# Source scan by flat scans: TensorE lays rows by feature in PSUM, GpSimd spreads flags, ScalarE spreads limits and turns rows back, VectorE scans

## The reference, cut to what matters

```
out = segment_sum(exp(-w)[:, None] * x[dst], src)      # layer 0: 64 features an edge
seg_sum = segment_sum(edge_attr_32, src)               # layer 1: 32 features an edge
seg_max = segment_max(edge_attr_32, src)               #          the same 32, maximum
h = relu(concat([seg_sum, seg_max, seg_mean, u]) @ W1 + b1) @ W2 + b2
```

## Time and profile before

| | us |
|---|---|
| median of 3 runs (9801.57 to 9804.97) | 9802.26 |
| the profiled execution | 9794.14 |
| its span | 9792.4 |
| its source scan (first flag comparison to last maximum, 2398.69 to 3061.24) | 662.5 |

### The profile page before, as it was taken

One profiled execution on the slowest core, in us unless ns is written; L12 is line 12 of the kernel. 1 busy time (PEld: TensorE's weight loads), 2 busy tenths in 40 slices (PEclk: granted clock), 3 DMA queues, 4 the chain that ended last, 5 costly groups with the idle time before them and its releaser, 6 DMA issues.

```text
span 9792.4 us, 48931 instructions
## 1 busy us (share of the span) xinstructions
PE 1437.4 (15%) x7747; PEld 1261.9 (13%) x7747; DVE 3669.9 (37%) x13437; ACT 2688.1 (27%) x3610; POOL 6744.4 (69%) x6983
## 2 busy tenths in 40 slices
PE   7544444441002200000001000000001000000000
PEld 6443333441001200000000000000001000000000
DVE  9766666664996311111111111111114222222225
ACT  0566666662000222222221222222220111111110
POOL 6677777775003577777777777777777777777775
PEclk6655555555555555555555555555555555555555
DMA  7445554454774122222222222222221222222222
GB/s 269 131 146 149 149 146 144 147 149 131 274 273 154 45 54 52 52 52 54 52 52 51 48 52 52 54 52 52 52 54 35 60 63 63 63 66 63 63 64 48
DMA packets 573558, 913.40 MB, mean 93 GB/s; under 512 B 335117, under 2 KB 351380, under 8 KB 547976
## 3 DMA queue, kind: packets, MB, share of 16 engines
q1 hardware_dynamic: 349752, 652.54, 20.0%
q0 software_dynamic: 223040, 258.35, 13.0%
q10 hardware_dynamic: 528, 0.15, 0.0%
HBM read 496.53 MB, written 414.02 MB: 93 GB/s over the span
## 4 chain that ended last, share of the span: by engine, by line
POOL 67%; issue 23%; DVE 7%; SPq 1%; DMA 1%; PE 1%; ACT 0%; DVEq 0%; POOLq 0%; ACTq 0%
POOL arena_a L690 45%; POOL by_src L638 16%; POOL arena_a L657 4%; DVE arena_a L1394 2%; DVE arena_a L1399 2%; POOL x_at_start L617 1%; SPq L415 1%; POOL adst_at_start L671 1%; DMA adst_at_start<-arena_a 0%; PE banks L1028 0%; DVE hrows L1284 0%; DVE cap_blk L1356 0%; DVE cap_blk L1357 0%; PE banks L952 0%; PE banks L1002 0%
## 5 line engine op out<-in xcount | busy, mean ns | idle before, releaser
L690 POOL DMA_INDIRECT arena_a<-table_c,decay x3136 | 2959.8, 944 | 1040.3 <-issue 954.8
L638 POOL DMA_INDIRECT by_src<-arena_b,idx_blk x1568 | 1555.4, 992 | 509.0 <-issue 476.7
L690 POOL DMA_INDIRECT arena_a<-table_at,decay x1568 | 1490.3, 950 | 477.8 <-issue 477.8
L1617 DVE COPY banks<-arena_a 128x64 f32<-128x64 f32 x194 | 52.7, 272 | 3346.3 <-ACT banks L753 3346.3
L753 ACT ACTIVATE banks<-arena_a 128x1024 f32<-128x1024 f32 x196 | 369.6, 1886 | 2999.0 <-DMA arena_a<-table_c,decay 2999.0
L733 ACT ACTIVATE arena_b<-same_dst 128x1024 f32<-128x1024 f32 (+1 forms) x294 | 312.9, 1064 | 1692.3 <-DVE arena_a L1755 1569.8
L742 ACT ACTIVATE arena_a<-arena_a 128x1024 f32<-128x1024 f32 (+1 forms) x294 | 597.9, 2034 | 3.9 <-DVE arena_a L1755 2.0
L976 PE MATMUL banks<-ident,chunk_end 128*64 128x128 f32 (+2 forms) x8 | 2.7, 442 | 3964.0 <-DVEq L1085 3964.0
L853 ACT ACTIVATE arena_b<-arena_a,decay 128x64 f32<-128x64 f32 x1568 | 468.1, 388 | 423.0 <-DMA by_src<-arena_b,idx_blk 423.0
L1710 DVE TENSOR_TENSOR arena_a<-arena_a 128x64 f32<-128x64 f32 x98 | 27.0, 275 | 1355.1 <-DMA arena_a<-table_at,decay 1355.1
L976 PEld LDWEIGHTS banks<-ident,chunk_end 128*64 128x64 f32 (+2 forms) x8 | 1.4, 239 | 3964.7 <-DVEq L1085 3964.7
(11 more groups left out here) (290 smaller groups left out, 5215.2 us busy)
## 6 DMA issues: line engine op xcount, KB each, us to landing
arena_a<-ids_rows SPq DMA_DIRECT2D x98, 1024.0 KB, 9.1
states_src<-arena_a SPq DMA_DIRECT2D x98, 1024.0 KB, 4.8
states_c<-arena_a SPq DMA_DIRECT2D x196, 512.0 KB, 2.6
hrows<-by_src SPq DMA_DIRECT2D x98, 776.0 KB, 6.1
states_at<-arena_a SPq DMA_DIRECT2D x98, 576.0 KB, 3.1
x_at_start<-arena_a SPq DMA_DIRECT2D x7, 7168.0 KB
arena_a<-x_at_start SPq DMA_DIRECT2D x98, 512.0 KB, 6.4
arena_a<-table_c,decay POOLq DMA_INDIRECT x3136, 2.4
```

What stands on the lines that cost most here:

```text
L638: pool.indirect_dma_start(out=by_src, out_offset=AT(ap=idx_blk[r][:, k:k + 1], axis=0), in_=rows[r][:, k, :], in_offset=None)\
L690: pool.indirect_dma_start(out=gb[r][:, k * w:(k + 1) * w], out_offset=None, in_=table[g], in_offset=AT(ap=src_i[:, n * J + k:n * J + k + 1 ...
```

## The change

The slots' chain of small steps becomes two flat scans a block, and four engines share the work:

- **TensorE** multiplies the block by the identity in four matmuls of 512 columns, whose operand is read with the slots inside and a step of 97 numbers between them. So a block lies in PSUM by feature, 128 features of 16 slots: 96 to sum, and the 32 attributes once more for the maxima. Two blocks fill the eight banks.
- **GpSimd** spreads the block's 15 flags over 96 features (`flags`, two buffers).
- **ScalarE** makes the caps, spreads them over 32 features (`caps_at`, two buffers), and behind the scans copies the block from `outs` (by feature, two buffers) to `runs` (by row, four buffers); it raises `state` now.
- **VectorE** compares the flags of the next block, puts the carries into slot 0 in PSUM, and scans 1536 and 512 elements.
- **SyncE** loads when a block's maxima are scanned and stores two blocks behind.

The diff, cut to its core:

```diff
+        def turned_src(h):
+            return banks[:, h * J * W01:(h + 1) * J * W01]
+        def slots_of(flat):
+            return flat.rearrange("p (f j) -> p f j", j=J)
...
+        late = carve(arena_a, [*((f"run{h}", J * W01) for h in range(R)), *((f"out{h}", J * W01) for h in range(2))])
+        late = carve(arena_b, [(f"flags{h}", J * WS) for h in range(2)] + [(f"caps{h}", J * E32) for h in range(2)])
...
@@ SyncE @@
                 for h in range(blocks):
                     if more:
                         if later(i) or h >= 2:
-                            sp.wait_ge(s("state"), i * R + h - 1)
+                            sp.wait_ge(s("src_maxed"), i * R + h - 1)
                         load(*((i, h + 2) if h < 2 else (i + 1, h - 2)))
-                    if later(i) or h:
-                        write_src(i * R + h - 1, (h - 1) % 2)
+                    if later(i) or h >= 2:
+                        write_src(i * R + h - 2, (h - 2) % R)
             def write_src(b, h):
                 sp.wait_ge(s("state"), b + 1)
                 sp.dma_start(rows_of(states["src"], W01)[:, bass.ds(b * (J * W01), J * W01)],
-                             st[h][:, 0:J * W01]).then_inc(s(f"stored{h}"), 16)
+                             runs[h][:, :]).then_inc(s(f"kept{h}"), 16)
...
@@ GpSimd @@
+            for n in range(NBLK):
+                pool.wait_ge(s("src_same"), n + 1)
+                if n >= 2:
+                    pool.wait_ge(s("src_summed"), n - 1)
+                pool.tensor_copy(slots_of(flags[n % 2])[:, :, 1:J], bf(mask_blk[:, n % 2, 1:J], WS))\
+                    .then_inc(s("src_spread"), 1)
...
@@ ScalarE @@
+            def caps_src(i, h):
+                q = h % 2
+                act.wait_ge(s("src_same"), i * R + h + 1)
+                if later(i) or h >= 2:
+                    act.wait_ge(s("src_maxed"), i * R + h - 1)
+                act.activation(cap_blk[:, q, :], mask_blk[:, q, :], ACT.Copy, bias=-1.0, scale=2.0)\
+                    .then_inc(s("cap_signs"), 1)
+                act.wait_ge(s("cap_signs"), i * R + h + 1)
+                act.activation(cap_blk[:, q, :], cap_blk[:, q, :], ACT.Copy, scale=HUGE).then_inc(s("src_capped"), 1)
+                act.wait_ge(s("src_capped"), i * R + h + 1)
+                act.activation(slots_of(caps_at[q])[:, :, 1:J], bf(cap_blk[:, q, 1:J], E32), ACT.Copy)\
+                    .then_inc(s("caps_spread"), 1)
+            def back_src(i, blocks=R):
+                for h in range(blocks):
+                    if h < R - 1 and (blocks == R or h < blocks - 1):
+                        caps_src(i, h + 1)
+                    elif blocks == R:
+                        caps_src(i + 1, 0)
+                    if later(i):
+                        act.wait_ge(s(f"kept{h}"), i * 16)
+                    rows = runs[h].rearrange("p (j f) -> p j f", f=W01)
+                    done = slots_of(outs[h % 2]).rearrange("p f j -> p j f")
+                    act.wait_ge(s("src_summed"), i * R + h + 1)
+                    act.activation(rows[:, :, 0:WS], done[:, :, 0:WS], ACT.Copy)
+                    act.wait_ge(s("src_maxed"), i * R + h + 1)
+                    act.activation(rows[:, :, WS:W01], done[:, :, WS:W01], ACT.Copy).then_inc(s("state"), 1)
+            caps_src(0, 0)
+            turns(act, back_src, TURNS)
+            back_src(TURNS, REST)
...
@@ TensorE @@
+            def turn_src(i, blocks=R):
+                for h in range(blocks):
+                    pe.wait_ge(s(f"tb_in{h}"), i * 16 + 16)
+                    if later(i) or h >= 2:
+                        pe.wait_ge(s("src_maxed"), i * R + h - 1)
+                    to = turned_src(h % 2)
+                    for b, f in enumerate((0, E32, D, D)):
+                        last = pe.matmul(to[:, b * J * E32:(b + 1) * J * E32], ident[:, :],
+                                         tb[h][:, :, f:f + E32].rearrange("p j f -> p f j"), start=True, stop=True)
+                    last.then_inc(s("src_turned"), 1)
...
@@ VectorE @@
+            for h in range(2):
+                link(v.memset(slots_of(flags[h])[:, :, 0:1], 0.0))
+                link(v.memset(slots_of(caps_at[h])[:, :, 0:1], -HUGE))
+            tell("src_same")
             def body(i, blocks=R):
                 for h in range(blocks):
...
+                    q, n = h % 2, (h + 1) % R
+                    if blocks == R or h < blocks - 1:
+                        v.wait_ge(s(f"tb_in{n}"), (i + (h + 1) // R) * 16 + 16)
+                        if later(i) or h:
+                            v.wait_ge(s("src_spread"), i * R + h)
+                            v.wait_ge(s("caps_spread"), i * R + h)
+                        for ins in same_src(n, tb[h][:, J - 1, TW - 1:TW]):
+                            pass
+                        ins.then_inc(s("src_same"), 1)
+                    v.wait_ge(s("src_turned"), i * R + h + 1)
+                    if later(i) or h:
+                        sums, maxima = (slots_of(turned_src(q))[:, f, 0] for f in (slice(0, WS), slice(WS, W01)))
+                        old = slots_of(outs[1 - q])
+                        v.wait_ge(s("src_summed"), i * R + h)
+                        v.scalar_tensor_tensor(out=sums, in0=old[:, 0:WS, J - 1], scalar=mask_blk[:, q, 0:1], in1=sums,
+                                               op0=ALU.mult, op1=ALU.add).then_inc(s("sum_carried"), 1)
+                        v.wait_ge(s("src_capped"), i * R + h + 1)
+                        v.wait_ge(s("src_maxed"), i * R + h)
+                        v.scalar_tensor_tensor(out=maxima, in0=old[:, WS:W01, J - 1], scalar=cap_blk[:, q, 0:1],
+                                               in1=maxima, op0=ALU.min, op1=ALU.max).then_inc(s("max_carried"), 1)
+                        v.wait_ge(s("sum_carried"), i * R + h)
+                    if later(i) or h >= 2:
+                        v.wait_ge(s("state"), i * R + h - 1)
+                    v.wait_ge(s("src_spread"), i * R + h + 1)
+                    v.tensor_tensor_scan(outs[q][:, 0:J * WS], flags[q], turned_src(q)[:, 0:J * WS], 0.0,
+                                         ALU.mult, ALU.add).then_inc(s("src_summed"), 1)
+                    if later(i) or h:
+                        v.wait_ge(s("max_carried"), i * R + h)
+                    v.wait_ge(s("caps_spread"), i * R + h + 1)
+                    v.tensor_tensor_scan(outs[q][:, J * WS:J * W01], caps_at[q], turned_src(q)[:, J * WS:J * W01], 0.0,
+                                         ALU.min, ALU.max).then_inc(s("src_maxed"), 1)
```

More of the change, by code:

```diff
@@ L314, in program @@
         tb = [late[f"tb{h}"].rearrange("p (j f) -> p j f", f=TW) for h in range(R)]
+        late = carve(arena_a, [*((f"run{h}", J * W01) for h in range(R)), *((f"out{h}", J * W01) for h in range(2))])
+        runs = [late[f"run{h}"] for h in range(R)]
+        outs = [late[f"out{h}"] for h in range(2)]
+        late = carve(arena_b, [(f"flags{h}", J * WS) for h in range(2)] + [(f"caps{h}", J * E32) for h in range(2)])
+        flags = [late[f"flags{h}"] for h in range(2)]
+        caps_at = [late[f"caps{h}"] for h in range(2)]
         late = carve(arena_a, [("st0", J * W01), ("st1", J * W01), *((f"g{r}", J * W3) for r in range(R)),
@@ L642, in node_states @@
             def node_states(g, w, o):
-                for h in range(2):
-                    pool.wait_ge(s(f"stored{h}"), upto(g, f"stored{h}") + 16 * NB)
+                if g == "src":
+                    for h in range(R):
+                        pool.wait_ge(s(f"kept{h}"), 16 * (TURNS + (h < REST)))
+                else:
+                    for h in range(2):
+                        pool.wait_ge(s(f"stored{h}"), upto(g, f"stored{h}") + 16 * NB)
                 pool.indirect_dma_start(out=fix_rows[:, 0:w], out_offset=None, in_=states[g],
@@ L1361, in _ @@
                 link(ins)
-            link(caps(0, 0))
-            link(caps(0, 1))
+            for h in range(2):
+                link(v.memset(slots_of(flags[h])[:, :, 0:1], 0.0))
+                link(v.memset(slots_of(caps_at[h])[:, :, 0:1], -HUGE))
+            tell("src_same")
             def body(i, blocks=R):
-                c2.turn(i)
                 for h in range(blocks):
-                    q = h % 2
-                    more = blocks == R or h < blocks - 1
+                    q, n = h % 2, (h + 1) % R
[19 more added lines that the diff above has]
+                        v.wait_ge(s("sum_carried"), i * R + h)
@@ L1375, in body @@
[L1375 to L1405, removed]
@@ L1406, in body @@
-                assert blocks < R or c2.k == c2.per, (c2.k, c2.per)
-            turns(v, body, NB * 2 // R)
-            body(NB * 2 // R, 2)
+                        v.wait_ge(s("max_carried"), i * R + h)
+                    v.wait_ge(s("caps_spread"), i * R + h + 1)
+                    v.tensor_tensor_scan(outs[q][:, J * WS:J * W01], caps_at[q], turned_src(q)[:, J * WS:J * W01], 0.0,
```

(6 more changed lines are left out.)

18 lines of the change are left out of this document (6 added, 12 removed).

## The result

| | us |
|---|---|
| before, median of 6 runs (9801.57 to 9805.53) | 9803.13 |
| after, median of 6 runs (9863.58 to 9872.88) | 9866.08 |
| after / before | 1.0064, interval 1.0053 to 1.0075 |
| the profiled execution of after (its span) | 9863.58 (9861.8) |
| its source scan (2399.20 to 3123.45, where before took 662.5) | 724.3 |

The change made the kernel 0.64% slower where 1.3% faster was predicted, and the time lies outside the range. The profiled executions differ by 69.4 us: the source scan is 61.7 us longer, it starts 0.5 us later, and the 7 us left lie behind it, where nothing was changed (the runs of after themselves spread over 9 us). The source scan ends with ScalarE's last copy here, and ended with VectorE's last maximum before.

What follows compares the result with a forecast made beforehand. VectorE was taken to bound the source scan at 6.75 us a block; after, 7.1 + 98 x 5.4 + 2.8 = 539 us against 662.5, 123 us less, so 9679 us predicted, range 9645 to 9765.

Steps and rivals of the forecast that it cites:

- the last of TensorE's part: Source scan, four fp32 matmuls a block: columns read 388 bytes apart cost nothing extra; 3.5 us at 2.4 GHz, hidden.
- The term: Source scan: time per block, the largest of 5.1, 5.1 and 5.2 us plus 0.2, so 5.4 us.
- the third rival: Source scan: TensorE stays at 1.2 GHz or reads stepped columns slower; 6.96 us a block, 9830 us in all; 10%.
- The clock: TensorE in the source scan: granted clock rises in block 1 and stays mostly up, above 0.9 in the stage.
- VectorE: Source scan: scans of 3.35 and 1.22 us, carries and flag comparisons; own pace 5.1 us a block, between 5.0 and 5.5.
- ScalarE: Source scan: five instructions a block, turning back 2.88 and 1.12 us, caps 0.6, two tiny ones 0.22 each; 5.1 us.
- GpSimd: Source scan: copying 1440 flag elements a block takes 2 us, between 1.35 and 2.95; hidden if under 5 us.
- The fourth rival: Source scan: GpSimd's copies are late (9738 us) or hold up the scans (9787 to 9944 us); 8%.
- The DMA floor: Source scan: loads of 776 KB and stores of 1024 KB a block need at least 5.2 us.
- The added 0.2 us: Source scan: allowance per block because three limits this close don't all hide one another.
- the first rival: Source scan: engines don't hinder each other and queues run full; 5.1 us a block, 9650 us in all; 12%.
- The ends: Source scan: 7.1 us before the first scan for the first block's matmuls, 2.8 us more for ScalarE's last turning.

Runs made afterwards that it cites:

- the last experiment: Sum scan cut from 1536 to 1024 elements, against the kernel reading neighbours and writing PSUM with the step: 10776.77 us, 201 below before on that chip.

## Why the prediction was wrong, step by step

- **The step that failed** is the last of TensorE's part: "No row has fp32 columns read 388 bytes apart; I take them at no extra cost." They cost 0.914 us a record against 0.43 to 0.44 for neighbours, so 7.31 us a block and not 3.5, and TensorE sets the pace instead of being hidden. The term was 5.4 us a block; 98 x (7.31 - 5.4) is 187 us, and 9866 less 9679 is 187. That the two agree to the microsecond is partly luck: the stage itself missed by 185 us (539 forecast, 724.3 measured), and the rest is small differences outside it and between the profiled executions and the medians.
- **Why it got through.** The unknown had no bound from above in the sum; it stood only as half a sentence in the third rival, tied to the clock. There it was priced at "6.96 us" a block, the row at the low clock, with 10%. Its second half named the mechanism, and 98 x 0.35 = 34 us lead from its 9830 to within 2 us of the 9866 measured. But the price was lucky: 6.96 us is what contiguous reading costs at the low clock, and no row priced a stepped one; that the two lie within 5% is chance. The prediction argued at length over the clock, which a reader of the earlier trace rows could settle either way, and took at no cost what no row covered. The range had to reach to 9870 for that reason alone. The chances don't add up there either: this rival alone has 10% and ends slower, yet "slower" got 0.09 in all.
- **The clock**: right. It rose within the first block and stayed at 1.00 for 700 us. But TensorE was busy all that time, so that "mostly up" was tried only in the easy case; in the kernel that reads neighbours, which idles a quarter of each block, it stayed at 1.00 as well.
- **VectorE**: right. Scans of 3.346 and 1.194 us (3.35 and 1.22 predicted), carries of 388 and 263 ns (360 and 240), and a pace of 5.007 us where nothing else is late (5.1, between 5.0 and 5.5).
- **ScalarE**: right in each term. 2866, 1063, 605, 216 and 207 ns (2.88, 1.12, 0.6, 0.22, 0.22); where neighbours are read it is busy for 445 us of 470, 4.74 us a block. The sum of 5.1 was too high, since neighbours overlap: in the last experiment its five instructions fit into 4.65.
- **GpSimd**: 1394 ns, at the low end of 1.35 to 2.95, below the 2 us taken and the estimate of 2.2, and hidden. It waits 5.9 us a block for its input in after (570.3 / 96), and 3.6 with neighbours read. The fourth rival fell for this form of scan.
- **The DMA floor** of 5.2 us was too high: in the version with neighbours the queues kept up with 5.007 us at a share of 0.98, and in the last experiment with 4.646 at 1.01. A share below 1 times a period is no floor; with the queues pressed harder the same bytes took less.
- **The added 0.2 us** for three close limits did not come: VectorE was busy for 469.66 of 470 us. So with the failed term mended the change is worth 163 us and not 123: the period is 0.39 us shorter than the 5.4 forecast (97 x 0.39 = 38), which is the first rival, *all hidden*, even a little better than its 5.1.
- **The ends**: 7.1 us for the first block's matmuls, measured 7.7 in after (5.9 with neighbours read); 2.8 us more at the end, measured 2.7 (3120.72, when L1464 ends, to 3123.45).

## What to carry to other kernels

Where a transfer or a matmul turns data, look first at how the operand is read from SBUF: with fp32, each 16-byte group should serve at least two columns, and if one side must be stepped, let it be the write to PSUM. An operation's price from a row holds only for its pattern of addresses; where no row has the pattern, bound it (here: twice) and carry the upper end into the range. And an engine that is busy for all of a window says nothing of the clock: compare the spacing of records at both levels.

## What the runs showed of the hardware

- Reads of TensorE's moving operand (the block; the identity is the weights), fp32, 512 columns a record, clock 1.00, by the spacing of weight loads: contiguous 0.43 us, step of two 0.45, of three 0.677, of four 0.90, of 97 0.914. At clock 0.50 contiguous took 0.85 and a step of 97 the same 0.92. So the cost of a group of 16 bytes doesn't follow the granted clock, and at the low clock the step costs only 8%.
- Writes to PSUM 64 bytes apart: 0.44 us a record, within 3% of contiguous (0.43).
- VectorE with both inputs in SBUF and GpSimd's copies take turns by whole instructions: the scans 1.27 and 1.96 times as long, GpSimd's copy 3.2 times, a carry of 32 elements 11 times (2947 against 263 ns). With one input in PSUM both keep their times (3346 and 1396 ns).
- The DMA queues moved 393 GB/s at a share of 1.01 over 430 us, loads of 776 KB and stores of 1024 KB in turn.
